# A blocked cross-attention on one core: a pair of scores, an exponent, a value copy and a maximum change their places in three queues

## The reference, cut to what matters

```
q = x1 @ Wq                       # x1: 128 x 256 after layernorm, Wq: 256 x 1024
k, v = split(x2 @ Wkv)            # x2: 12544 x 256, 16 heads of 64 each
attn = softmax(q k^T / 8)         # per head, 128 x 12544
out = (attn @ v) @ Wo + bo
```

## Time and profile before

| | |
|---|---|
| median of 3 runs | 1557.54 us (1556.43 to 1558.33) |
| the profiled execution's own time | 1554.04 us |
| its span in the trace | 1552.3 us, mean granted PE clock 0.975 |
| busy over the span | PE 94%, PEld 81%, DVE 70%, ACT 53%, POOL 39% |
| first stage | from the start to about 1163 us; its 224 steps from 35.6 us on |

### The profile page before, as it was taken

The page is one execution under the profiler, slowest core; times in us unless marked ns, Lnnn a source line. Parts: engine busy times, 40 slices in busy tenths (PEclk is TensorE's granted clock), DMA queues, the critical chain, the costliest instruction groups (busy, mean ns, idle before and its releaser), DMA issues. The chain is left out here.

```text
span 1552.3 us, 24869 instructions
## 1 busy us (share of the span) xinstructions
PE 1461.3 (94%) x9105; PEld 1258.2 (81%) x9105; DVE 1080.9 (70%) x2053; ACT 828.1 (53%) x1578; POOL 604.7 (39%) x519
## 2 busy tenths in 40 slices
PE   6999999999999999999999999999977889999379
PEld 5888888888888888888888888888865778888248
DVE  6777777777777777777777777777775356666764
ACT  2655665556665565665565666565651255555121
POOL 6343433434343434343434343433300256665330
PEclk9999999999999999999999999999997899999779
DMA  5000000000000000000000000000007112220600
GB/s 183 1 8 18 1 25 1 25 1 25 1 25 1 25 1 25 1 24 1 24 1 24 1 24 1 1 1 1 1 28 312 63 70 71 71 71 24 284 1 4
DMA packets 9102, 57.18 MB, mean 37 GB/s; under 512 B 2121, under 2 KB 2720, under 8 KB 7969
## 3 DMA queue, kind: packets, MB, share of 16 engines
q1 hardware_dynamic: 8992, 55.73, 9.6%
HBM read 55.60 MB, written 0.13 MB: 36 GB/s over the span
## 5 line engine op out<-in xcount | busy, mean ns | idle before, releaser
L468 DVE TENSOR_TENSOR pT<-ps,pT 128x896 fp32r<-128x896 f32 x224 | 244.5, 1092 | 204.2 <-ACT pT L378 204.2
L305 POOL CAST V<-Vraw 128x512 fp32r<-128x512 f32 x189 | 115.8, 613 | 653.1 <-ACT Vraw L384 552.3
L378 ACT ACTIVATE pT<-ps 128x896 fp32r<-128x896 f32 x224 | 206.1, 920 | 179.1 <-PE ps L540 178.3
L384 ACT COPY Vraw<-ps 128x512 f32<-128x512 f32 x189 | 111.0, 587 | 265.3 <-PE ps L522 265.3
L306 POOL TENSOR_TENSOR V<-Vraw,V 128x512 fp32r<-128x512 f32 x189 | 242.3, 1282 | 15.1
L422 DVE TENSOR_REDUCE nmx<-ps 128x1 f32<-128x896 f32 x224 | 242.0, 1080 | 0.0
L365 ACT ACTIVATE prob<-ps,nm 128x896 f32<-128x896 f32 x224 | 224.2, 1001 | 0.0
L598 PE MATMUL ps<-ident,prob 128*128 128x128 f32 x1568 | 214.5, 277 | 8.6 <-ACT prob L365 4.5
L553 PEld LDWEIGHTS ps<-pT,V 128*128 128x128 f32 x1568 | 215.0, 188 | 8.3 <-issue 0.3
L553 PE MATMUL ps<-pT,V 128*128 128x256 f32 x1568 | 220.2, 280 | 0.0
L598 PEld LDWEIGHTS ps<-ident,prob 128*128 128x128 f32 x1568 | 167.5, 140 | 17.1 <-ACT prob L365 9.2
(11 more groups left out here) (307 smaller groups left out, 2398.6 us busy)
## 6 DMA issues: line engine op xcount, KB each, us to landing
raw<-in_ctxT SPq DMA_DIRECT2D x14, 896.0 KB, 4.5
d_raw<-in_ctxT SPq DMA_DIRECT2D x14, 896.0 KB, 4.6
w<-in_w SPq DMA_DIRECT2D x2, 4096.0 KB, 18.3
wg<-in_wg SPq DMA_DIRECT2D x1, 4352.0 KB, 27.5
wu<-in_wu SPq DMA_DIRECT2D x1, 4352.0 KB, 16.8
wd<-in_wd SPq DMA_DIRECT2D x1, 4352.0 KB, 26.7
e_ea<-in_alog SPq DMA_DIRECT2D x1, 2048.0 KB, 7.3
wq<-in_wq SPq DMA_DIRECT2D x1, 1024.0 KB, 5.3
```

The source lines that it names most:

```text
L305: link(pool, nc.gpsimd.tensor_copy(v_high(g, i), by_head(Vraw[:, j % 2, :])), "pool_chain")
L378: nc.scalar.activation(pT[u % 2][:, :, 0, :], pT_ps, ACT.Copy).then_inc(sem("pTh_ready"), 1)
L468: nc.vector.tensor_tensor(pT[u % 2][:, :, 1, :], pT_ps, pT[u % 2][:, :, 0, :].bitcast(F32), ALU.subtract).then_inc(sem("pTl_ready"), 1)
```

## The change

Three moves, all in `stage_context`; no instruction is added or removed.

- PE: in odd steps the pair of scores goes from behind the transposes of step u to a place ahead of them, right behind `exp_done` (the waits on `pTl_ready` and `u_added` stay ahead of the transposes and so come behind the scores).
- ACT: `exp_step(u + 1)` goes from behind the copy of the value piece to a place ahead of it.
- DVE: the two maxima of each odd step become one per step, `max_step(u + 1)` in every step from u = 1 on, ahead of the wait on `pTh_ready` and the low probabilities.

```
@@ -376,14 +376,14 @@
                     act.wait_ge(sem("p_turned"), u + 1)
                     nc.scalar.activation(pT[u % 2][:, :, 0, :], pT_ps, ACT.Copy).then_inc(sem("pTh_ready"), 1)
+                    if u + 1 < steps:
+                        exp_step(u + 1)
                     if u in v_steps:
                         j = v_steps.index(u)
                         act.wait_ge(sem("v_done"), NT + j + 1)
                         if j >= 2:
                             act.wait_ge(sem("v_split"), j - 1)
                         nc.scalar.copy(Vraw[:, j % 2, :], ps[:, 6, :]).then_inc(sem("vraw_ready"), 1)
-                    if u + 1 < steps:
-                        exp_step(u + 1)
                     if u + AHEAD < steps:
                         high_parts(u + AHEAD)
@@ -464,19 +464,17 @@
                     if 1 <= u and u - 1 + AHEAD < steps:
                         low_parts(u - 1 + AHEAD)
+                    if u >= 1 and u + 1 < steps:
+                        max_step(u + 1)
                     dve.wait_ge(sem("pTh_ready"), u + 1)
                     nc.vector.tensor_tensor(pT[u % 2][:, :, 1, :], pT_ps, pT[u % 2][:, :, 0, :].bitcast(F32),
                                             ALU.subtract).then_inc(sem("pTl_ready"), 1)
-                    if u % 2 == 1 and u + 1 < steps:
-                        max_step(u + 1)
                     if u >= 2:
                         update_sums(u - 2)
                     if u >= H0:
                         dve.wait_ge(sem("u_added"), u - H0 + 1)
                     nc.vector.tensor_scalar(den[:, h:h + 1], den[:, h:h + 1], al[:, b:b + 1],
                                             rs[:, b:b + 1], ALU.mult, ALU.add)
-                    if u % 2 == 1 and u + 2 < steps:
-                        max_step(u + 2)
                     if u >= 1:
                         add_parts(u - 1)
@@ -590,6 +588,9 @@
                     pe.wait_ge(sem("exp_done"), u + 1)
+                    if u % 2 == 1 and u + 1 < steps:
+                        pe.wait_ge(sem("kl_ready"), u + 3)
+                        scores((u + 1) // 2)
                     if u >= 1:
                         pe.wait_ge(sem("pTl_ready"), u)
@@ -601,9 +602,6 @@
                         mm = turn_sums(u - 2)
                     mm.then_inc(sem("p_turned"), 1)
-                    if u % 2 == 1 and u + 1 < steps:
-                        pe.wait_ge(sem("kl_ready"), u + 3)
-                        scores((u + 1) // 2)
                     if u in v_steps:
```

## The result

The changed kernel takes 1653.24 us (median of 4, 1650.36 to 1654.43) against 1557.53 (4 runs), a ratio of 1.062, 95% interval 1.061 to 1.0635. The forecast was 1672, range 1640 to 1700. The spans of the two profiled executions are 1648.7 and 1552.3 us, 96.4 apart.

The account below looks back on a forecast made before the run. PE's own stream was taken to bound the kernel. 27 groups of eight steps at +4.41 us (119) less 4.5 in the last eight steps, net +114.5 on 1554.0, gave 1668.5; with 3.5 for the median, 1672 us, range 1640 to 1700.

Parts of the forecast that it names:

- ACT's queue: Exponent ahead of value copy: the weighted sum waits, PE standing 0.40 us in each step with a value piece.
- The late maximum in even steps: DVE's maximum, behind `Kl` and `add_parts`, frees `al` 3.47 us after the weighted sum starts, against 2.94 by the ACT copy.
- In odd steps: Odd steps with a value piece: 6.32 us instead of 5.96, +0.36, with the maximum early by 0.47.
- The PE edge: Scores right behind the weighted sum: edge between nothing and 0.31 us, scores starting 1.11 us after the sum's first load.
- The clock: With new PE gaps of 0.4 to 0.9 us in nearly each step, the granted clock holds at 1.00.
- the last eight steps: Odd steps' transposes no longer wait for a maximum; a pair takes about 8.2 us instead of 9.72, -4.5 in all.
- even step with a value piece: Even step from one weighted sum to the next: 5.29 us instead of 4.36, +0.93.
- step without one, and the odd one behind it: Step without a value piece (u % 8 = 6) plus the next odd step: 10.01 us instead of 9.47, +0.54.
- the mark L: The first weight load of the weighted sum on PE, from which the distance to the next such load was worked out.
- the first: Rival: the even maximum is not late, only ACT's queue counts, 67 us in all, 1620 us; chance 0.06.
- the second: Rival: not slower, the value copy still comes in time and the last eight steps win 4.5, 1553 us; chance 0.04.
- the third: Rival: the clock falls to the 1.2 GHz level for a tenth of the time, 108 us more, 1780 us; chance 0.04.

Follow-up runs that it names:

- e1: The changed kernel with ACT's part undone, the value copy ahead of the exponent again: 1548.07 us, ratio 0.9948.
- e3: The changed kernel with both maxima of a pair in the odd step, ahead of the low probabilities: 1597.59 us.
- e10: The kernel before, with the changed order of scores and maximum in the last eight steps only: 1555.66 us, ratio 1.0002.
- e4: The changed kernel with DVE's part undone, the odd step's maximum behind the low probabilities as before: 1944.86 us.
- e8: e2 with the weighted sum ahead of the key piece in steps without a value piece: 1536.19 us, ratio 0.986.
- e2: The kernel before with scores early and both maxima in the odd step ahead of the low probabilities, ACT unchanged: 1543.64 us, ratio 0.9914.

## Why the prediction was right, and where its terms were off

The side and the cause hold. **ACT's queue** was predicted as the price, and e1, which undoes it alone, gives back all of it. **The late maximum in even steps** was predicted as the longer of the two chains there; the trace of after has `al` 0.03 or 0.04 us behind L425 in each even step of the groups, and e3 takes 0.56 us of the step away. **In odd steps** the maximum was predicted to be early by 0.47: in the trace L425 ends at 614.53 + 0.21 and `al` starts at 615.17, with no wait. **The PE edge** that the trace of before didn't show cost as much as the one I chose. **The clock** stayed at 1.00 in the groups, as rows 6 suggested.

The sum was too large by 18 us (114.5 against 96). Two misses of opposite sign are in it: the groups were priced 23 us too high and the last eight steps 5 us too low. By terms:

| term | predicted | measured |
|---|---|---|
| even step with a value piece | 5.29 | 5.18 |
| odd step with a value piece | 6.32 | 6.19 |
| step without one, and the odd one behind it | 10.01 | 3.28 + 6.58 = 9.86 |
| a group against before | +4.41 | +3.54 |
| 27 groups | +119 | +95.6 |
| the last eight steps | -4.5 | +0.6 |

The step without a value piece and the odd one behind it, in the changed kernel:

```profile
639.71 0.89 PEld L551 LDWEIGHTS ps<-pT,V 128*128 128x128 f32 x7 [0.42 <-ACT Vraw L386]
642.99 0.98 PEld L551 LDWEIGHTS ps<-pT,V 128*128 128x128 f32 x7
...
649.57 0.89 PEld L551 LDWEIGHTS ps<-pT,V 128*128 128x128 f32 x7 [0.41 <-ACT Vraw L386]
```

The term that was mis-sized is the distance from the mark L. I took the distances behind the weighted sum from rows in which PE comes to it at full flow (1.22 us to `add_parts`, 1.11 to the scores). There the first load of the sum runs 0.20 us ahead of its first matmul (616.01 and 616.21 in rows 2). In the changed kernel the sum starts after a wait, and load and matmul start together: its seven loads take 0.89 instead of 0.98, `add_parts` starts 1.14 after the first of them and the scores 1.02. Each chain crosses this place once per step, and 0.08 or 0.09 of the 0.11 and 0.13 that are missing lie there.

The other is the last eight steps. The prediction says that an odd step's transposes stop waiting for the maximum; in rows 5 it is the even steps' transposes that wait. It also gives no working for "about 8.2 by the same chains". Its chain for an even step without a value piece is 3.35, and in this one the step takes 4.30 (the next sum begins at 1236.31); the odd step behind it takes 4.82. So the miss lies in the even step, and there in DVE's list. Timeline of the changed kernel, where steps 217 and 218 meet:

```profile
1232.01 0.98 PEld L551 LDWEIGHTS ps<-pT,V 128*128 128x128 f32 x7
...
1233.17 0.53 ACT L356 CAST Kh<-ps 128x448 fp32r<-128x448 f32 x1
...
1233.59 0.42 DVE L430 TENSOR_REDUCE osb<-ps 128x128 f32<-128x256 f32 x1
...
1234.30 0.29 DVE L445 TENSOR_TENSOR U<-U,rden 128x128 f32<-128x128 f32 x1
...
1234.51 0.61 DVE L415 TENSOR_TENSOR Kl<-ps,Kh 128x448 fp32r<-128x448 f32 x1
...
1235.17 0.30 PEld L509 LDWEIGHTS ps<-cTh,wkh 128*128 128x128 f32 x2 [0.71 <-DVE Kl L415]
```

`add_parts` (L430) starts 1.58 us behind the sum and not 1.22, because DVE is still at the low probabilities and the sums. Then, in odd steps from 211 on, DVE scales two finished heads (`scale_sums`, L442 to L445), and `Kl` stands behind that: 0.92 us behind `add_parts` and not 0.35. Together these are 0.93 of the 0.95 us. The high key part `Kh` had ended at 1233.70, 0.8 us before `Kl` began, so ACT's order isn't what holds `Kl` here, as I took it to be in the expectation of e10. The pair takes 9.10 us (9.72 before), not 8.2, and the pair ahead of it wins nothing (9.74 in both kernels). And further back, where no key pieces are left to fill PE, the scores wait 2.42 us for the exponent, and the transposes behind them run at the lower clock (granted 0.50):

```profile
1246.85 0.19 PEld L531 LDWEIGHTS ps<-Kh,qh 64*128 64x128 f32 x2 [2.42 <-ACT prob L365]
...
1248.79 1.35 PEld L599 LDWEIGHTS ps<-ident,prob 128*128 128x128 f32 x7 [0.54 <-issue]
```

e1 has the same lists in these eight steps and the same wait of 2.42 us, but its clock stays at 1.00, and there the step with these scores takes 5.55 us from sum to sum instead of 6.80. So 1.3 of the 5.1 us that this term was off are the clock, which falls in one execution and not in the other.

Of the rivals, the first was wrong because of `add_parts` (e3 shows what it would have given), the second because the value copy doesn't fit in, and the third didn't occur in the groups of the changed kernel, though e4 shows its mechanism in a kernel with longer waits.

## What to carry to other kernels

When an instruction is moved forward in one engine's list, price what it is moved ahead of: here a 0.6 us copy with 0.19 us to spare was put behind 1.2 us of exponent, on an engine half idle. Reorders on several engines have to be priced together: early scores cost 150 us alone and gain 8 us together with the early maximum (e1), while the early exponent costs in every combination; the best kernels here take the scores and both maxima early but leave the copy first. Where a full engine shows a wait with ready work right behind it, as with the key piece and the weighted sum, that swap is worth a try: it gained 7 us (e8 against e2), where putting the exponent first, on an engine with slack, gained nothing.

## What the runs showed of the hardware

Gaps are given here as the time without a weight load. The granted clock holds at 1.00 through gaps of 0.96 us in each even step with a value piece (after), and of 1.2 to 2.0 us in the last eight steps of the kernel before (rows 5 and 6 have those of 1.23). It fell behind gaps of 2.42 us (after, e10) and 2.93 us (e4), for a few us each time. It didn't fall behind each such gap: in e1 the same gap of 2.42 us left it at 1.00, and in e4 the loads at 609.16 run at full speed. In e4 the lower clock cost some 70 us on top of the 311 of the waits themselves. The Trainium skill (TensorE: Matmul & The Clock Gate, "A second HAM failure mode: psum-queue depth-cycling") has frequent small idle times between groups of matmuls make the clock go to and fro between its levels; the changed kernel, with a gap of 0.4 or 0.96 us in nearly each step and a clock of 1.00 in its groups, does not show it.

The seven loads of a weighted sum take 0.98 us behind a key piece at full flow, where the first of them runs 0.20 us ahead of its matmul, and 0.89 us where it doesn't: after a wait (605.60), and also without one, behind transposes (e8, 624.15). So a distance measured from the first load is 0.08 or 0.09 us too long for a kernel in which that load waits.
